# Last expert feed-forward of a gated cross-attention stack: tokens sorted by expert through DRAM, 96 blocks of 128 rows for the two chosen experts

## Chip, cores and metric

The kernel runs on one core of one Trainium2 chip. The metric is the device time of one execution in microseconds. Engine names are those of the profile: PE (TensorE), DVE (VectorE), ACT (ScalarE), POOL (GpSimd) and SP, which issues DMAs.

## What is computed

The input x has 32 x 128 = 4096 rows of 128 numbers, all fp32. Four layers follow each other, each a gated cross-attention and a gated feed-forward of another kind. Only the last feed-forward is touched:

```
h = rmsnorm(layernorm(x)) * norm_w
logits = h @ gate_w.T + gate_b                 # 8 experts
vals, idx = top_k(logits, 2);  wts = softmax(vals)
t1 = einsum('td,efd->tef', h, mlp1_w) + mlp1_b # 256 wide: gate and linear halves interleaved
act = min(g, 7) * sigmoid(1.702 * min(g, 7)) * (clip(l, -7, 7) + 1)
y = einsum('tei,edi->ted', act, mlp2_w) + mlp2_b
x = x + tanh(g_ffn[3]) * (layernorm(x) + sum of wts * y over the two chosen experts)
```

The reference computes y for all eight experts and then takes two of them.

## The kernel before

x stays in SBUF for the whole program, as 32 tiles of 128x128; a group is four tiles (512 rows), so there are NG = 8 groups. Every engine has its own program, written out by hand stage after stage, in the order of `todo`: attention 0, feed-forward 0, attention 1, feed-forward 1 with the token attention, feed-forward 2, attention 2, feed-forward 3. An engine runs its instructions in order, and waits on semaphores that others raise (`wait_ge`). `walk` writes the first and last pair of groups out and loops over those between. The stages meet at the counter `x_written`, which VectorE raises.

In the last feed-forward (`feed_forward3` of each engine) the loops run over 8 groups, and in each over 8 experts. A group's rows are normalised (VectorE L1159 to L1182, POOL L439 to L522), POOL multiplies by the rms factor (L485), TensorE turns the tiles (L977), ScalarE copies them (L704), TensorE makes the logits (L1000) and VectorE picks the two best with 13 small operations and makes the weights (`top2`, L1411 to L1449). Per expert TensorE makes the gate half (L1090) and the linear half (L1093) for 512 rows; VectorE takes the gate half (L1615), ScalarE copies the linear half (L774), VectorE clips it (L1618), ScalarE makes the sigmoid (L779), POOL makes both products (L476, L493), TensorE the down product (L1009), and VectorE adds it to x times the row's weight, zero for six of eight experts (L1460). The biases of the down product are added for all experts at once (L1104, L1623). All the weights lie in SBUF since attention 2 began.

SP's queue carries plain DMAs alone: `load_ctx` (L341), `spread` (L355, L359), the token loads of `token_attention` (L410) behind the spreads of attention 1, and, once `x_written` passes each quarter, four stores of the output (L424). POOL issues no DMA.

## Time and profile before

| | |
|---|---|
| median of 3 runs | 1883.38 us (1877.07 to 1887.72) |
| the profiled execution | 1879.95 us |
| its span, first to last instruction | 1877.0 us |
| granted TensorE clock, mean | 0.921 of 2.4 GHz |
| DMA packets, bytes | 62833, 63.59 MB |

A fp32 product shows as two matmul instructions (passes), a transpose or a bf16 product as one. Busy times of TensorE are modelled at their ends, so of passes back to back the spacing tells more than the mean. A row of a timeline gives start and length in us, and for an instruction that ended an idle time that idle time and who released it. "SPq" is SP's own queue of orders; a DMA's length there is the time to issue it, and the time to landing stands in the list of DMA issues.

### The profile page before, as it was taken

What the parts mean: (1) busy time and instruction counts of PE and PEld (TensorE: products, weight loads), DVE (VectorE), ACT (ScalarE), POOL (GpSimd) and SP (SyncE); (2) the same over time, 40 slices, a digit from 0 to 9 for tenths busy, and PEclk for the clock granted to TensorE, in tenths of its full rate; (3) what the DMA queues carried; (4) which work ended last, traced back from release to release, by engine and by line L of the source; (5) the groups of instructions that cost most, each with busy time, mean ns of one, the idle gap of its engine ahead of it and who ended that gap; (6) DMA issues with size and microseconds to landing.
All of it is one profiled execution on the core that took longest, in us unless ns stands there. A gap on an engine that the chain in (4) does not pass through costs nothing. (4 is left out here: it accounts for less than half of the span.)

```text
span 1877.0 us, 33463 instructions
## 1 busy us (share of the span) xinstructions
PE 1519.4 (81%) x10824; PEld 925.0 (49%) x10824; DVE 1393.7 (74%) x3602; ACT 781.4 (42%) x1314; POOL 511.7 (27%) x559
## 2 busy tenths in 40 slices
PE   3888894488889799889889899935788899778787
PEld 1455552255555465555555455522355556445454
DVE  5777776667776547888887888876567667698997
ACT  1555563145556423334333333422356556333332
POOL 0000000000000003354353443553000000477786
PEclk9998897589999899999999999975999999899998
DMA  7444530254253000000000000004053532000000
GB/s 170 68 70 57 71 53 1 34 145 70 41 69 55 1 1 1 6 1 7 6 0 6 0 7 18 1 0 73 9 70 43 71 47 35 1 1 12 11 12 12
DMA packets 62833, 63.59 MB, mean 34 GB/s; under 512 B 6064, under 2 KB 57776, under 8 KB 62128
## 3 DMA queue, kind: packets, MB, share of 16 engines
q1 hardware_dynamic: 62704, 61.99, 20.3%
q8 instruction: 66, 1.08, 0.2%
q14 instruction: 63, 0.52, 0.1%
HBM read 22.12 MB, written 2.10 MB: 13 GB/s over the span
## 5 line engine op out<-in xcount | busy, mean ns | idle before, releaser
L1208 DVE TENSOR_REDUCE neg_max<-bank 128x4 f32<-128x512 f32 x384 | 260.4, 687 | 114.2 <-PE bank L839 108.0
L653 ACT ACTIVATE probs<-bank 128x512 f32<-128x512 f32 x384 | 229.2, 598 | 237.7 <-PE bank L862 235.3
L1009 PEld LDWEIGHTS bank<-room,area 128*128 128x128 f32 x2048 | 254.7, 199 | 100.2 <-issue 63.0
L439 POOL TENSOR_SCALAR rstd_a<-meanvar 128x4 f32<-128x4 f32 x64 | 17.0, 266 | 1023.5 <-DVE meanvar L1164 1023.5
L1009 PE MATMUL bank<-room,area 128*128 128x128 f32 x2048 | 264.0, 284 | 31.2 <-DVE area L1489 17.3
L729 ACT ACTIVATE work<-bank 128x512 f32<-128x512 f32 (+1 forms) x192 | 114.6, 597 | 358.0 <-PE bank L1034 353.1
L1038 PE MATMUL bank<-xT,room 128*128 128x512 f32 (+1 forms) x384 | 201.1, 606 | 16.2 <-DVE area L1489 16.1
L837 PE MATMUL bank<-mask_b,ident_b 128*128 128x512 bf16 x384 | 158.0, 412 | 66.7 <-DVE neg_max L1208 55.3
L1489 DVE TENSOR_TENSOR area<-work,bank 128x512 f32<-128x512 f32 (+1 forms) x192 | 128.8, 679 | 99.3 <-PE bank L1038 78.2
L1034 PE MATMUL bank<-xT,room 128*128 128x512 f32 (+1 forms) x384 | 198.3, 598 | 0.0
L551 POOL TENSOR_TENSOR prod<-mask_i,work 128x128 f32<-128x128 f32 (+3 forms) x128 | 126.6, 1022 | 156.7 <-DVE mask_i L1550 156.7
L839 PE MATMUL bank<-k_rows,q_rows 96*128 96x256 bf16 x768 | 157.2, 288 | 0.0
L862 PE MATMUL bank<-q_rows,k_rows 128*128 128x128 bf16 x1536 | 156.5, 227 | 0.0
L862 PEld LDWEIGHTS bank<-q_rows,k_rows 128*128 128x128 bf16 x1536 | 124.3, 102 | 62.2 <-issue 15.5
L858 PE MATMUL bank<-ident_b,mask_b 128*128 128x512 bf16 x384 | 154.4, 402 | 0.0
L646 ACT ACTIVATE q_rows<-bank 32x512 bf16<-32x512 bf16 x192 | 113.3, 590 | 95.9 <-PE bank L849 91.7
L874 PE MATMUL bank<-probs,v_aug 128*32 128x128 f32 x3072 | 151.1, 290 | 1.2 <-ACT probs L653 1.0
L1460 DVE SCALAR_TENSOR_TENSOR x<-bank,comb,x 128x128 f32<-128x128 f32 (+1 forms) x512 | 143.0, 339 | 5.5 <-PE bank L1009 3.4
L538 POOL TENSOR_TENSOR probs<-h,work 128x128 f32<-128x128 f32 (+3 forms) x128 | 114.4, 924 | 83.2 <-DVE probs L1530 73.9
L1038 PEld LDWEIGHTS bank<-xT,room 128*128 128x128 f32 (+1 forms) x384 | 68.6, 182 | 117.9 <-issue 85.9
L1182 DVE TENSOR_SCALAR xn<-x,meanvar,rstd 128x128 f32<-128x128 f32 (+1 forms) x192 | 75.6, 456 | 55.2 <-POOL rstd L441 55.0
L839 PEld LDWEIGHTS bank<-k_rows,q_rows 96*128 96x128 bf16 x768 | 79.1, 103 | 55.2 <-issue 13.5
(164 smaller groups left out, 2402.6 us busy)
## 6 DMA issues: line engine op xcount, KB each, us to landing
q_rows<-area SPq DMA_DIRECT2D x144, 128.0 KB
k_rows<-area SPq DMA_DIRECT2D x288, 64.0 KB
ctxT<-ctx_t SPq DMA_DIRECT2D x24, 256.0 KB, 8.0
mask_i<-mask SPq DMA_DIRECT2D x8, 256.0 KB, 8.5
work<-ctx_in SPq DMA_DIRECT2D x8, 256.0 KB, 2.8
out<-x SPq DMA_DIRECT2D x4, 512.0 KB, 3.2
room<-w_down SPq DMA_DIRECT2D x1, 1536.0 KB, 13.8
room<-w_gate SPq DMA_DIRECT2D x1, 1408.0 KB, 6.3
```

Of the source, the lines that this page charges most:

```text
L653: act.activation(probs[j].rearrange("p a b -> p (a b)"), T_BANK[j % 2][:], ACT.Exp).then_inc(exp_done, 1)
L837: pe.matmul(dst[:], ident_b[:], bcast(mask(b, t), 4), start=True, stop=False)
L839: mm = pe.matmul(dst[:, 256 * i:256 * i + 256], q_rows[b][SCORE_ROWS, 2 * j + i, tok], k_rows[b][SCORE_ROWS, :, 2 * j + i, tok], start=Fal ...
L858: pe.matmul(dst[:], mask(b, t), bcast(ident_b[:], 4), start=True, stop=False)
L862: mm = pe.matmul(dst[:, i * P:(i + 1) * P], k_rows[b][:, i % 2, 2 * j + i // 2, tok], q_rows[b][:, 2 * j + i // 2, tok], start=False, stop ...
L874: mm = pe.matmul(O_BANK[32 * i:32 * i + 32, j * P:(j + 1) * P], v_aug[b][:, t, 4 * j + i, :], probs[j][:, i, :], start=True, stop=True)
L1009: mm = pe.matmul(dst[:, t * P:(t + 1) * P], h[:, t * P:(t + 1) * P], w, start=i == 0, stop=i == len(terms) - 1)
L1034: pe.matmul(S_BANK[(3 * e + c) % 2][0:size, :], wg[:, e, at:at + size], xT[b][:], start=True, stop=True).then_inc(gate_filled, 1)
L1038: pe.matmul(T_BANK[(3 * e + c) % 2][0:size, :], wu[:, e, at:at + size], xT[b][:], start=True, stop=True).then_inc(up_filled, 1)
L1208: dve.tensor_reduce(neg_max[:, 4 * j:4 * j + 4], S_BANK[j % 2][:].rearrange("p (h k) -> p h k", h=4), AX.X, ALU.max, negate=True).then_inc ...
L1460: ins = dve.scalar_tensor_tensor(xt, src[:, t * P:(t + 1) * P], comb[cb][:, t, e:e + 1], xt, ALU.mult, ALU.add)
L1489: dve.tensor_tensor(hidden[e % 2][0:size, c, :], work[(3 * e + c) % 2][0:size, :], T_BANK[(3 * e + c) % 2][0:size, :], ALU.mult).then_inc( ...
```

## The change

Only the last feed-forward is rewritten; four DMAs are added before the token attention, and one constant at the start of the program.

- The 4096 rows are worked on in NCH = 4 chunks of 1024 rows (TC = 8 tiles). For each chunk VectorE chooses the two experts of each row (`choose`, 13 chained operations), TensorE counts ranks (`ranks`, 17 bf16 products with a triangular and an all-ones matrix), and VectorE turns them into row addresses and a table of 24 blocks: each block's expert and its place (`put`, 4 chained operations to the addresses, 15 more to the table).
- POOL scatters the chunk's normalised rows to a DRAM buffer `moe_rows` with 16 indirect DMAs of 128 rows, in two halves with the norm chain of a later group between them (`scatter`). Each expert has a region of 1152 rows per chunk; another 3072 rows take the blocks that are empty. The buffer has 4 x 12288 rows of 512 B and is cleared by four DMAs (`clear_rows`) that SP issues before the token loads.
- Then 24 rounds k run, six per chunk, each on a "quad" of four blocks. SP reads each block's address from SBUF into a register (`value_load`) and loads the block (`load`); TensorE turns the blocks (`turn_blk`), reads the four experts' offsets into registers (`value_load` in `up`), multiplies by the weights at these offsets, adds biases with a one-hot bf16 product, turns the hidden rows (`turn_hidden`) and makes the down product (`down_blk`); ScalarE copies between PSUM and SBUF and makes the sigmoid; VectorE clips and multiplies. SP stores the four result blocks to the places they came from (`store`). The two products that POOL made are now VectorE's.
- When a chunk's blocks are stored, POOL gathers them back in 16 indirect DMAs (`gather`; the order on POOL is scatter 0, 1, 2, gather 0, scatter 3, gather 1, 2, 3), and VectorE adds them to x with their weights (`combine3`, 16 operations a chunk).
- The product with the rms factor moves from POOL to VectorE (`group_norm`). The up and down biases are loaded after attention 2 has ended, and split into three bf16 parts by VectorE in eight chained operations (`split_bias`) ahead of the first norm.

The code around the rounds, of SP, POOL, ScalarE, TensorE and VectorE in turn; removed lines are those of the stage described above:

```diff
+TC = 2 * TG
+NCH = NT // TC
+CAP = TC * P + P
+QUAD = 4
+NQ = 6
+NBLK = QUAD * NQ
+REGION = E * CAP + NBLK * P
...
+            def clear_rows():
+                sp.wait_ge(zeros_made, 1)
+                for c in range(NCH):
+                    sp.dma_start(moe_rows[c * REGION:(c + 1) * REGION].rearrange("(p i a) d -> p i (a d)", p=P, a=4),
+                                 bcast(zeros[:], REGION // (4 * P))).then_inc(zeroed, 16)
...
+            def feed_forward3():
+                sp.wait_ge(x_written, NT * 6)
+                sp.dma_start(bias_f[BIAS_ROWS], bias3).then_inc(experts_loaded, 16)
+                sp.wait_ge(zeroed, 16 * NCH)
+                rows_at = {}
+                def load(k):
+                    c, q = divmod(k, NQ)
+                    if q == 0:
+                        sp.wait_ge(table_ready, c + 1)
+                        sp.wait_ge(scattered[c], 16 * 2 * TC)
+                    if k >= 4:
+                        sp.wait_ge(blk_turned, k - 3)
+                    waits_apart(sp)
+                    for j in range(QUAD):
+                        at = sp.value_load(block_i[0:1, c, QUAD * q + j:QUAD * q + j + 1], min_val=0,
+                                           max_val=NCH * REGION - P)
+                        rows_at[k, j] = at
+                        sp.dma_start(blk[k % 4][:, j, :], moe_rows[bass.ds(at, P), :]).then_inc(blk_loaded[k % 4], 16)
+                def store(k):
+                    sp.wait_ge(blk_out, k + 1)
+                    waits_apart(sp)
+                    for j in range(QUAD):
+                        sp.dma_start(moe_rows[bass.ds(rows_at[k, j], P), :], work[2 + k % 2][:, j * P:(j + 1) * P]
+                                     ).then_inc(blk_stored[k % 2], 16)
+                for k in range(NCH * NQ):
+                    load(k)
+                    if k >= 3:
+                        store(k - 3)
+                for k in range(NCH * NQ - 3, NCH * NQ):
+                    store(k)
 
...
-                    lambda: (attention(2, True), load_experts3()), lambda: attention(2, False), lambda: None)
+                    lambda: (attention(2, True), load_experts3()), lambda: attention(2, False), feed_forward3)
...
+                def scatter(c, half):
+                    pool.wait_ge(placed, c + 1)
+                    pool.wait_ge(h3_ready, 2 * c + half + 1)
+                    if c == 0 and half == 0:
+                        pool.wait_ge(zeroed, 16 * NCH)
+                    waits_apart(pool)
+                    for t in range(TG):
+                        for k in range(2):
+                            o = 2 * (TG * half + t) + k
+                            pool.indirect_dma_start(
+                                moe_rows, bass.IndirectOffsetOnAxis(place_i[:, c, o:o + 1].bitcast(mybir.dt.uint32), 0),
+                                h_all[:, TC * c + TG * half + t, :], None).then_inc(scattered[c], 16)
+                def gather(c):
+                    for b in range(2):
+                        pool.wait_ge(blk_stored[b], 16 * QUAD * NQ // 2 * (c + 1))
+                    if c >= 2:
+                        pool.wait_ge(combined, c - 1)
+                    waits_apart(pool)
+                    for o in range(2 * TC):
+                        pool.indirect_dma_start(
+                            y_taken[c % 2][:, o, :], None, moe_rows,
+                            bass.IndirectOffsetOnAxis(place_i[:, c, o:o + 1].bitcast(mybir.dt.uint32), 0)
+                        ).then_inc(gathered[c], 16)
 
                 rms_norm(0)
+                rms_norm(1)
+                rms_norm(2)
+                for c in range(3):
+                    scatter(c, 0)
+                    rms_norm(2 * c + 3)
+                    scatter(c, 1)
+                    if c < 2:
+                        rms_norm(2 * c + 4)
+                gather(0)
+                scatter(3, 0)
+                scatter(3, 1)
+                for c in range(1, NCH):
+                    gather(c)
 
...
+                def take_out(k):
+                    act.wait_ge(blk_down, k + 1)
+                    if k >= 2:
+                        act.wait_ge(blk_stored[k % 2], 16 * QUAD * (k // 2))
+                    act.activation(work[2 + k % 2][:], R_BANK[:], ACT.Copy).then_inc(blk_out, 1)
...
+                take_blk(0)
+                for k in range(NCH * NQ):
+                    c, q = divmod(k, NQ)
+                    if k + 1 < NCH * NQ:
+                        take_blk(k + 1)
+                    if c < 2:
+                        if q == 1:
+                            turned(2 * c + 4)
+                        if q == 3:
+                            turned(2 * c + 5)
+                    gate(k)
+                    if k >= 1:
+                        take_hidden(k - 1)
+                    if k >= 2:
+                        take_out(k - 2)
+                    if c < 2 and q == 4:
+                        gap_weight(c + 2)
+                take_hidden(NCH * NQ - 1)
+                take_out(NCH * NQ - 2)
+                take_out(NCH * NQ - 1)
 
...
+                def turn_blk(k, turns):
+                    pe.wait_ge(blk_loaded[k % 4], 16 * QUAD * (k // 4 + 1))
+                    if k:
+                        pe.wait_ge(blk_taken, k)
+                    pe.wait_ge(f_read, FB[3] + turns)
+                    for j in range(QUAD):
+                        mm = pe.transpose(X_BANK[:, j * P:(j + 1) * P], blk[k % 4][:, j, :], ident[:])
+                    mm.then_inc(blk_turned, 1)
+                weights_at = {}
+                def up(k):
+                    c, q = divmod(k, NQ)
+                    for j in range(QUAD):
+                        b = QUAD * q + j
+                        weights_at[k, j] = pe.value_load(expert_i[0:1, c, b:b + 1], min_val=0, max_val=3 * P * (E - 1))
+                    pe.wait_ge(blk_taken, k + 1)
+                    for half, (bank_, free, filled) in enumerate(((S_BANK, glu_taken, blk_glu),
+                                                                  (T_BANK, blk_lin_taken, blk_lin))):
+                        if k >= 2:
+                            pe.wait_ge(free, k - 1)
+                        for j in range(QUAD):
+                            dst = bank_[k % 2][:, j * P:(j + 1) * P]
+                            pe.matmul(dst, turned_blk[k % 2][:, j * P:(j + 1) * P],
+                                      room[:, bass.ds(weights_at[k, j] + half * P, P)], start=True, stop=False)
+                            hot = expert_hot[BIAS_ROWS, c, QUAD * q + j:QUAD * q + j + 1].to_broadcast([32 * PARTS, P])
+                            mm = pe.matmul(dst, hot, bias_b[BIAS_ROWS, half * P:(half + 1) * P], start=False, stop=True)
+                        mm.then_inc(filled, 1)
+                def turn_hidden(k):
+                    pe.wait_ge(blk_hidden, k + 1)
+                    if k:
+                        pe.wait_ge(blk_hid_taken, k)
+                    for j in range(QUAD):
+                        mm = pe.transpose(O_BANK[:, j * P:(j + 1) * P], hid[k % 2][:, j * P:(j + 1) * P], ident[:])
+                    mm.then_inc(blk_hid_turned, 1)
+                def down_blk(k):
+                    c, q = divmod(k, NQ)
+                    pe.wait_ge(blk_hid_taken, k + 1)
+                    if k:
+                        pe.wait_ge(blk_out, k)
+                    for j in range(QUAD):
+                        dst = R_BANK[:, j * P:(j + 1) * P]
+                        hot = expert_hot[BIAS_ROWS, c, QUAD * q + j:QUAD * q + j + 1].to_broadcast([32 * PARTS, P])
+                        pe.matmul(dst, hot, bias_b[BIAS_ROWS, 2 * P:3 * P], start=True, stop=False)
+                        mm = pe.matmul(dst, work[k % 2][:, j * P:(j + 1) * P],
+                                       room[:, bass.ds(weights_at[k, j] + 2 * P, P)], start=False, stop=True)
+                    mm.then_inc(blk_down, 1)
+                for c in range(2):
+                    turned(2 * c, 0)
+                    turned(2 * c + 1, 0)
+                    logits(c)
+                    ranks(c)
+                turn_blk(0, 4)
+                for k in range(NCH * NQ):
+                    c, q = divmod(k, NQ)
+                    turns = min(2 * c + 4 + (q >= 2) + (q >= 4), 2 * NCH)
+                    if k + 1 < NCH * NQ:
+                        turn_blk(k + 1, turns if q < NQ - 1 else min(2 * c + 6, 2 * NCH))
+                    up(k)
+                    if c < 2 and q in (1, 3):
+                        turned(2 * c + 4 + (q == 3), k + 2)
+                    if k >= 1:
+                        turn_hidden(k - 1)
+                    if k >= 2:
+                        down_blk(k - 2)
+                    if c < 2:
+                        if q == 3:
+                            logits(c + 2)
+                        if q == 5:
+                            ranks(c + 2)
+                turn_hidden(NCH * NQ - 1)
+                down_blk(NCH * NQ - 2)
+                down_blk(NCH * NQ - 1)
 
...
+                def gated(k):
+                    dve.wait_ge(blk_glu, k + 1)
+                    if k >= 2:
+                        dve.wait_ge(blk_sig, k - 1)
+                    dve.tensor_scalar(glu[k % 2], S_BANK[k % 2][:], 7.0, None, ALU.min).then_inc(glu_taken, 1)
+                    dve.wait_ge(blk_lin, k + 1)
+                    dve.tensor_scalar(lin[k % 2], T_BANK[k % 2][:], 8.0, -6.0, ALU.min, ALU.max).then_inc(blk_lin_taken, 1)
+                    dve.wait_ge(blk_lin_taken, k + 1)
+                    step(dve.tensor_tensor(lin[k % 2], lin[k % 2], glu[k % 2], ALU.mult))
...
+                for k in range(NCH * NQ):
+                    c, q = divmod(k, NQ)
+                    gated(k)
+                    if c < 2:
+                        if q == 0:
+                            group_norm(2 * c + 5)
+                        if q == 1 and c == 0:
+                            group_stats(6)
+                        if q == 4:
+                            choose(c + 2)
+                        if q == 5:
+                            put(c + 2)
+                            if c == 0:
+                                group_norm(6)
+                                group_stats(7)
+                    hide(k)
+                    if c >= 2 and q == NQ - 1:
+                        combine3(c - 2)
+                combine3(2)
+                combine3(3)
 
...
```

## Rows read from the trace of the kernel before

**Rows 1.** The page, first part: busy time, share of the span, instructions.

```profile
PE 1519.4 (81%) x10824; PEld 925.0 (49%) x10824; DVE 1393.7 (74%) x3602; ACT 781.4 (42%) x1314; POOL 511.7 (27%) x559
```

**Rows 2.** Busy time by stretch, last feed-forward: us, each engine (count), clock, DMA.

```profile
1606.00:1877.00 271.00, 209.25 (x936) 131.71 (x936) 232.59 (x648) 86.89 (x153) 196.31 (x184) 0.92 0.03 8
```

**Rows 3.** Groups by line and form, 1605 to 1877 us: busy, mean ns, idle before.

```profile
L476 POOL TENSOR_TENSOR probs<-probs,work 128x512 f32<-128x512 f32 x64 | 82.6, 1290 | 49.5 <-DVE probs L1618 49.5
...
L1009 PE MATMUL bank<-room,area 128*128 128x128 f32 x512 | 74.2, 291 | 13.9 <-POOL area L493 13.9
...
L1615 DVE TENSOR_SCALAR work<-bank,cols 128x512 f32<-128x512 f32 x64 | 47.5, 742 | 4.0 <-DVE comb L1449 2.0 <-DVE route L1420 0.9 <-PE bank L1090 0.8
...
L1618 DVE TENSOR_SCALAR probs<-probs 128x512 f32<-128x512 f32 x64 | 42.1, 658 | 11.5 <-ACT probs L774 11.4
L779 ACT ACTIVATE work<-work 128x512 f32<-128x512 f32 x64 | 40.1, 627 | 87.5 <-DVE work L1615 85.0 <-POOL area L493 2.5
...
L1460 DVE SCALAR_TENSOR_TENSOR x<-bank,comb,x 128x128 f32<-128x128 f32 x128 | 35.8, 339 | 3.9 <-PE bank L1009 3.4
```

**Rows 4.** Timeline where the last feed-forward begins: start, length, instruction, idle before.

```profile
1605.71 0.29 DVE L1253 TENSOR_TENSOR x<-x,tgbo 128x128 f32<-128x128 f32 x1
...
1607.42 0.23 POOL L439 TENSOR_SCALAR rstd_a<-meanvar 128x4 f32<-128x4 f32 x1 [78.08 <-DVE meanvar L1164]
...
1609.96 0.75 DVE L1600 SCALAR_TENSOR_TENSOR x<-xn,gates,x 128x512 f32<-128x512 f32 x1
1611.05 1.04 POOL L485 TENSOR_TENSOR h<-xn,rms 128x512 f32<-128x512 f32 x1 [0.17 <-POOL rms L522]
...
1614.27 1.88 PE L1000 MATMUL bank<-wr,xT 128*128 128x8 f32 x8 [0.84 <-ACT xT L704]
...
1616.18 0.19 DVE L1411 TENSOR_TENSOR route<-bank,rows 128x32 f32<-128x32 f32 x1 [5.47 <-PE bank L1000]
...
1618.71 0.19 DVE L1437 TENSOR_TENSOR route<-rows,route 128x32 f32<-128x32 f32 x1
```

**Rows 5.** How orders to the DMA queue are issued: ns, min/median/max, by line.

```profile
L341 SPq DMA_DIRECT2D ctxT<-ctx_t x24: 336/350/543, 4.9 to 1532.4; - x24
L341 SPq FUSED_REGOPS  x12: 43/46/56, 126.3 to 1532.2; - x12
...
L359 SPq DMA_DIRECT2D k_rows<-area x288: 602/613/1720, 27.8 to 1566.0; - x144
```

**Rows 6.** The page, last part: DMA issues, KB each, us from issue to landing.

```profile
room<-w_down SPq DMA_DIRECT2D x1, 1536.0 KB, 13.8
...
ident<-consts_in SPq DMA_DIRECT2D x1, 64.0 KB, 2.5
...
wr<-w_router SPq DMA_DIRECT2D x1, 4.0 KB, 1.6
```

**Rows 7.** Timeline of TensorE: passes back to back at full and at half clock.

```profile
1592.33 0.39 PE L862 MATMUL bank<-q_rows,k_rows 128*128 128x128 bf16 x4
...
1592.55 0.61 PE L886 MATMUL bank<-ident,heads_t 128*128 128x128 f32 x4
...
1701.68 1.05 PE L1009 MATMUL bank<-room,area 128*128 128x128 f32 x8
...
1869.90 2.08 PE L1009 MATMUL bank<-room,area 128*128 128x128 f32 x8 [1.87 <-POOL area L493]
```

**Rows 8.** Busy time by stretch, a thinly used stretch after the first feed-forward.

```profile
301.00:378.00 77.00, 25.24 (x103) 13.30 (x103) 50.83 (x116) 8.72 (x14) 4.24 (x7) 0.51 0.18 25
```

**Rows 9.** Timeline of the end: last expert add and last output store.

```profile
1872.01 1.12 DVE L1460 SCALAR_TENSOR_TENSOR x<-bank,comb,x 128x128 f32<-128x128 f32 x4 [2.64 <-PE bank L1009]
...
1873.36 0.37 SPq L424 DMA_DIRECT2D out<-x  x1
```

**Rows 10.** Timeline: token loads issued, and their first reader on POOL.

```profile
595.03 1.00 SPq L410 DMA_DIRECT2D work<-ctx_in  x2
...
723.12 3.31 POOL L538 TENSOR_TENSOR probs<-h,work 128x128 f32<-128x128 f32 x4 [1.23 <-DVE h L1182]
```

More of the change, by code:

```diff
@@ L51 @@
 CH1 = [(0, 128), (128, 128), (256, 96)]
+TC = 2 * TG
[5 more added lines that the diff above has]
+REGION = E * CAP + NBLK * P
+PARTS = 3
+BIAS_ROWS = slice(0, 32 * PARTS)
 MASKED = -float(2.0 ** 100)
@@ L496, in feed_forward3 @@
-                rms_norm(0)
-                def body(gp, first, last):
-                    for gr, b, is_first, left in groups(gp, first, last):
-                        for e in range(E):
-                            if e >= 1:
-                                hide(E * gr + e - 1, e - 1, DB3 + 9 * gr + e - (1 if e >= 3 else 2))
-                            elif not is_first:
-                                hide(E * gr - 1, 7, DB3 + 9 * gr - 2)
-                            if e == 1 and left >= 1:
-                                rms_norm(gr + 1)
-                            products(E * gr + e, e)
@@ L1114, in feed_forward3, with turned, logits @@
-                walk(pe, body)
-                for e in (E - 2, E - 1):
-                    finish(E * NG + e - E, e, DB3 + 9 * NG + e - E)
+                pe.wait_ge(experts_loaded, 16 * 8)
+                pe.wait_ge(bias_split, 1)
+                def turned(p, blocks):
+                    if blocks:
+                        pe.wait_ge(blk_taken, blocks)
+                    turn(3, p)
+                def logits(c):
+                    for half in range(2):
+                        pe.wait_ge(f_read, FB[3] + 2 * c + half + 1)
+                        if c and half == 0:
+                            pe.wait_ge(chosen_ready, c)
+                        for t in range(TG):
+                            at = (TG * half + t) * E
+                            mm = pe.matmul(N_BANK[:, at:at + E], xT[half][:, t * P:(t + 1) * P], wr3[:],
+                                           start=True, stop=True)
+                    mm.then_inc(logits_filled, 1)
```

354 lines of the change are left out of this document (212 added, 142 removed).

## Prediction

> **What bounds the kernel now.** I read the page's busy shares first: over the whole run TensorE leads with 81% and VectorE follows with 74% [rows 1]. The change lies in the last feed-forward, so next I read busy time by stretch. That stage begins when attention writes its last row at 1606.0 us and ends with the span at 1877.0: 271 us, in which VectorE is busy for 232.6, TensorE for 209.3, POOL for 196.3 and ScalarE for 86.9 [rows 2, 4]. VectorE comes closest to a bound: per group of 512 rows and expert it takes the gate half (64 x 0.742 = 47.5 us in all), clips the other half (42.1) and adds the expert's output to x (256 x 0.339, twice the 35.8 of the row shown, = 72) [rows 3]. All of it goes with 8 groups x 8 experts = 64 rounds, so a round costs 271/64 = 4.2 us. The median of three runs is 1883.4 us; the profiled execution took 1880.0, its span 1877.0. I add to this execution, so my figure is some 3 us below what the median would give. A difference of 0.5% (9 us) is about what a measurement can tell from none.
>
> **What the change does to engine time.** The 64 rounds go. In their place 24 rounds ("quads") of four 128-row blocks run, and around them stand a sort and a gather. Per quad TensorE issues 8 one-pass fp32 transposes, 12 fp32 products of two passes each, and 12 bf16 bias products. Eight fp32 passes take 1.05 us, one of them some 0.29, so a pass adds (1.05-0.29)/7 = 0.108; four bf16 passes take 0.39, so 0.054 each [rows 3, 7]. That is 32 x 0.108 + 12 x 0.054 = 4.1 us at the full clock and 8.2 at the half clock, where the same eight passes take 2.08 [rows 7]. VectorE: 0.742 x 2 from PSUM, two 512-wide SBUF products at some 0.66 (L1618's mean), waits 0.4: 3.2 us. Its adds fall from 256 to 64, which saves 65 us. By busy time alone the stage would shrink. What decides is what a quad waits for.
>
> **The loop through the SP queue.** SP's program is load(k), then store(k-3). TensorE's round k begins with the turn of quad k+1, so needs load(k+1). On SP that stands behind store(k-3), which waits for ScalarE's copy of quad k-3. That copy reads what TensorE made as the *last* work of round k-1 (down_blk). So four input buffers exist, yet the load that round k needs first is ordered only after round k-1 has ended. From round 3 to round 22, 20 times, the legs add up:
> - SP leg. Hand-over and copy, 0.3 + 0.6 + 0.2 = 1.1 us (the copy by L779's 0.627 [rows 3]). Four stores: a contiguous store or load of 128 runs is issued in 0.35 us at L341, plus two address instructions of 0.046, so 0.45 each, 1.8 in all [rows 5]. The strided spreads take 0.61, the upper bound. Four loads, each behind a register load from SBUF: 4 x (v + 0.45). Landing of the last: a 64 KB load took 2.5 us, a 4 KB load 1.6; I take 2.2 [rows 6].
> - The register load v (value_load) is not in this trace. It cannot be less than a register operation, 0.05 us, and I bound it above by a whole 4 KB transfer, 1.6 us [rows 5, 6]. The nearest row is the issue of one DMA, also sequencer work that reaches across the chip, 0.35; the value must come back besides, so I take 0.5. SP leg: 1.1 + 1.8 + 3.8 + 2.2 = 8.9 us.
> - TensorE leg. Wait 0.2; four register loads of its own, 4 x 0.5 = 2.0, in its queue behind the turn; addresses 0.3; array work between 4.1 and 8.2. With 4 to 8 us of work in a round of 18 the array is thinly used; at a third busy the granted clock was 0.51, nearly always the lower level, 1.2 GHz [rows 8]. The work comes in bursts, though, so I take the middle, 6.2. Leg: 8.7 us.
>
> A round is 17.6 us; 20 rounds are 352 us. ScalarE and VectorE (3.2 us, in rounds with routing some 13) fit beneath it at no cost; if the loop were short, they and TensorE would set some 7 us.
>
> The Trainium skill ("DMA: Bandwidth & Descriptors", Latency and other measured facts) gives a floor of about 600 ns for loading a register; no row here shows it. By it v is 0.6, and eight such loads in 20 rounds make the forecast 16 us later.
>
> **Before the first quad.** Bias: its DMA is issued only when attention is done (2.7 us by [rows 6]) and VectorE splits it in eight chained steps of some 0.55: 7.1 us. Two groups normalised in turn: from 1605.9 to 1610.7, plus a product of 0.7: 5.6 each, 11.2 [rows 4]. Transposes, copy and logits: 4.1 us from 1612.1 to 1616.2 before, 4.5 for two. Choice: 13 chained operations took 2.7 us, 3.1 for twice the width [rows 4]. Ranks (17 bf16 products, cold) 2.4 and places 1.5. So rows have places at 1606 + 30 = 1636. Then POOL scatters 16 times, with a norm chain of 3.6 us between [rows 4]. An indirect DMA is not in this trace: below, 0.35 as SP's issue; above, two passes of a 128x512 tensor by POOL, 2.6; I take one pass, 1.3 (L476) [rows 3, 5]. 16 x 1.3 + 3.6 = 24.4, landing 2.5: 1663. Load(0) 3.8 + 2.2, load(1) 3.8: round 0 starts at 1673, 67 us into the stage. Rounds 0 to 2 have loads ahead: 7 + 8 + 9 = 24 us.
>
> **After it.** Round 23 and the last turn and down 13; copy, stores, landing 5.4; gather(3) 16 x 1.3 + 2.5 = 23.3; combine 16 x 0.339 + 0.5 = 5.9; output store 3.7, as from 1873.3 to the end of the span [rows 3, 9]. Together 51 us. The other 96 indirect DMAs (125 us at 1.3) lie beside the quads. Both 16s on the path move by 32 us for each microsecond of price.
>
> The Trainium skill (same page, Anatomy of one DMA) gives 2.0 us fixed plus bytes by 436 GB/s for a DMA from GpSimd, mostly completion, which overlaps when many are in flight. If it did not overlap, 2.15 instead of 1.3 in 32 of them would be 27 us more.
>
> **Elsewhere.** Clearing 4 x 12288 rows of 512 B writes 25.2 MB from SP, ahead of the token loads now issued at 595 us and first read at 723 [rows 10]. At the rate of the 1536 KB load (13.8 us, with its start) it is 226 us, 98 late [rows 6]; an idle queue should do better, so I take nothing, upper bound 98. The extra constant at the start and the turns inside quads of chunks 0 and 1: 5 us. All other stages stay.
>
> **Sum.** 67 + 24 + 352 + 51 + 5 = 499 us against 271: +228. 1880 + 228 = **2108 us**, 12% slower. With every term low (v 0.05, full clock, landing 1.6) a round is 11.2 us and the time 1980; with v 1.6, strided issue and half clock it is 31 and 2376.
>
> **Rivals.**
> - *Faster: the loop costs nothing.* Place: SP's store(k-3). If outputs were ready when SP reaches it, quads would go at the engines' pace, TensorE 4.1 + 4v. With v 0.05, full clock, cheap scatter (0.4) a quad takes 5.4: 57 + 130 + 35 = 222 us, 1831 in all. Decision point: 147 + 20R = 271 gives R = 6.2 us a round. Against it: the legs above exceed that even at their lowest, 11.2; it needs the order of the queues to be other than read. 4%. The same without the loop but at v 0.5: some 7 us a quad, near 1885, 3%.
> - *POOL sets the pace.* At 3.5 us an indirect DMA, POOL has 128 x 3.5 + 35 = 483 us of work and the 32 on the path add 70: about 2180. For it: POOL is slow per operation here (0.23 us for four elements a lane, rows 4). The Trainium skill ("SBUF — State Buffer", the "DVE blocks DMA" trap) adds that VectorE's fast mode can keep GpSimd from writing descriptors. 8%.
> - *The clearing stalls the tokens*: up to +98, so 2206, with the rest as forecast. 7%.
> - *It does not do what it says*: the static 96 blocks run whether full or empty, so work never falls below 24 quads. That is in the sum.
>
> **Chances.** Forecast (R from 13 to 23) 78%, POOL 8, clearing 7, no loop 7 (faster 4, the same 3). Range: R 13 to 23 gives 2016 to 2216; the bounds of v and of the rivals widen it to 1985 to 2265. Faster by over 0.5% 0.04, within 0.5% 0.03, slower 0.93.
>
> **What would show it.** In the changed profile: SP's longest total wait is its stores on ScalarE's output copy; TensorE waits about 20 times some 9 us for blocks' landing; the mean clock of the stage is nearer 0.6 than 0.92; quads follow each other at 16 to 19 us; register loads on SP and TensorE near 0.5 us; first block load issued near 1663. The prediction is wrong if TensorE's waits for blocks are short, or if POOL's queue is solid between the first scatter and the last gather, or if a stage before 1606 us has moved by over 10 us.

## The result, and the profile after

The changed kernel takes 2114.09 us (median of 4 runs, 2110.17 to 2115.08) against 1885.37 us before (4 runs on the same chip): ratio 1.1218, 95% interval 1.1192 to 1.1245. The forecast was 2108 us, 12% slower. The profiled execution took 2113.85, its span 2112.1.

First the page's first part and the busy time of the last feed-forward in three stretches: attention's last row (1604.6 us) to just before the first store of a quad, the waiting rounds, the rest. They answer to [rows 1, 2].

```profile
PE 1522.4 (72%) x11108; PEld 980.0 (46%) x11108; DVE 1308.5 (62%) x3375; ACT 761.5 (36%) x1271; POOL 467.3 (22%) x552
...
core 0: us, PE busy (x) PEld busy (x) DVE busy (x) ACT busy (x) POOL busy (x), PEclk, DMA share, GB/s
1604.60:1693.00 88.40, 32.51 (x194) 29.00 (x194) 49.60 (x182) 10.75 (x17) 54.58 (x74) 0.55 0.12 38
1693.00:2060.00 367.00, 164.38 (x920) 143.31 (x919) 78.96 (x182) 50.81 (x83) 82.05 (x86) 0.66 0.15 44
2060.00:2112.00 52.00, 15.95 (x108) 14.45 (x108) 18.70 (x59) 5.44 (x9) 15.10 (x16) 0.63 0.29 81
```

Attention ends within 1.4 us of where it did before, so the earlier stages, clearing included, did not move. The stage takes 507.5 us where it took 271. It is no longer short of an engine: VectorE is busy for 147 us where it was for 233, POOL for 152 where it was for 196. In the middle stretch nobody is busy for half of the time, TensorE included (164 of 367 us). So the time lies in waits. This is the table of waits over 1693 to 2060 us (who waited, for whom, total, times, longest), and the same for SyncE's queue:

```profile
DVE area L1881 <- PE bank L1264: 238.0, 19, 14.9
ACT area L866 <- PE bank L1244: 180.3, 20, 9.6
PEld bank L1244 <- DMA k_rows<-moe_rows: 171.9, 20, 9.2
PE bank L1244 <- DMA k_rows<-moe_rows: 168.5, 20, 9.0
```

```profile
SPq L91 <- ACT work L879: 249.2, 20, 16.8
```

Every engine waits, each for the next one round the ring: VectorE for TensorE, TensorE for the loaded blocks (20 times, 8.4 us on average), SyncE for ScalarE's copy of the output (20 times). Only the order of the queues tells which link is superfluous. One round in time (TensorE's bf16 bias products and weight loads, POOL and some VectorE lines left out):

```profile
1806.38 0.44 PE L1284 MATMUL bank<-room,work 128*128 x2
...
1806.86 0.60 ACT L879 ACTIVATE work<-bank 128x512 f32<-128x512 f32 x1 [0.74 <-PE bank L1284]
1807.60 1.78 SPq L481 DMA_DIRECT2D moe_rows<-work  x4
...
1810.19 3.64 SPq L475 DMA_DIRECT2D k_rows<-moe_rows  x4
...
1815.38 1.11 PE L1244 MATMUL bank<-ident,k_rows 128*128 128x128 f32 x4 [8.56 <-DMA k_rows<-moe_rows]
1816.54 0.69 ACT L866 ACTIVATE area<-bank,cols 128x512 f32<-128x512 f32 x1 [9.08 <-PE bank L1244]
1818.16 0.79 PE L1261 MATMUL bank<-room,area 128*128 x2 [1.66 <-ACT area L866]
...
1826.38 0.60 ACT L879 ACTIVATE work<-bank 128x512 f32<-128x512 f32 x1 [0.26 <-PE bank L1284]
1827.12 1.78 SPq L481 DMA_DIRECT2D moe_rows<-work  x4
```

The reader is to see one chain in which only one link works at a time: down projection (L1284), copy (L879), four stores (L481), four loads (L475), landing, turn (L1244), up projection (L1261), down projection. TensorE stands still for 8.56 us of it. From the stores at 1694.0 to those at 2069.0 there are 20 such rounds in 375.0 us, 18.75 each; 17.6 was forecast.

The reads of registers were the price the trace of before did not have. This is what lines 472 (SyncE) and 1253 (TensorE) issue, ns as min/median/max:

```profile
L472 SPq TENSOR_LOAD <-k_rows x96: 263/268/494, 1659.2 to 2055.1; - x96
L472 SPq FUSED_REGOPS  x96: 152/152/185, 1659.7 to 2055.4; - x96
L472 SPq SEQ_ASSERT  x96: 18/18/37, 1660.0 to 2055.6; - x96
```

```profile
L1253 PEldq TENSOR_LOAD <-k_rows x96: 293/298/578, 1669.8 to 2067.3; - x96
```

### The profile page after: what moved, and what is told of

Read it like the earlier page. It is cut to its first block and busy times, and to the rows that moved or that the text cites. A ratio compares the mean times of both kernels' runs of the same rounds, so it can differ in the third digit from the quotient of the medians.

```text
span 2112.1 us, 34421 instructions
## 1 busy us (share of the span) xinstructions
PE 1522.4 (72%) x11108; PEld 980.0 (46%) x11108; DVE 1308.5 (62%) x3375; ACT 761.5 (36%) x1271; POOL 467.3 (22%) x552
## 3 DMA queue, kind: packets, MB, share of 16 engines
q0 software_dynamic: 4096, 8.40, 1.3%
## 5 line engine op out<-in xcount | busy, mean ns | idle before, releaser
L1139 PEld LDWEIGHTS bank<-room,area 128*128 128x128 f32 x1536 | 187.3, 198 | 56.4 <-issue 41.7
L1139 PE MATMUL bank<-room,area 128*128 128x128 f32 x1536 | 191.0, 283 | 16.8 <-DVE area L1686 16.8
L1881 DVE TENSOR_SCALAR area<-bank 128x512 f32<-128x512 f32 x24 | 16.6, 691 | 265.4 <-PE bank L1264 265.4
L1244 PE MATMUL bank<-ident,k_rows 128*128 128x128 f32 x96 | 25.7, 420 | 180.4 <-DMA k_rows<-moe_rows 180.4
L1261 PE MATMUL bank<-room,area 128*128 x384 | 116.6, 448 | 38.4 <-ACT area L866 23.8
```

The costliest lines, as they stand in the source:

```text
L1139: mm = pe.matmul(dst[:, t * P:(t + 1) * P], h[:, t * P:(t + 1) * P], w, start=i == 0, stop=i == len(terms) - 1)
L1261: pe.matmul(dst, turned_blk[k % 2][:, j * P:(j + 1) * P], room[:, bass.ds(weights_at[k, j] + half * P, P)], start=True, stop=False)
```

## Experiments

Four groups of kernels ran, each group on one chip, and the chips turned out to differ in one thing (below), so I compare rounds within a profile as well as times. A round is the distance between two turns of a quad (the line of `pe.transpose(X_BANK..., blk...)`), and I give the median of the 20 waiting ones, with their mean where it differs. The numbers in brackets behind a time are its ratio to the kernel before, measured on the same chip, and the 95% interval of that ratio.

### One part of the loop at a time

**The store one round later.** SyncE only:

```
-                    if k >= 3:
-                        store(k - 3)
-                for k in range(NCH * NQ - 3, NCH * NQ):
+                    if k >= 4:
+                        store(k - 4)
+                for k in range(NCH * NQ - 4, NCH * NQ):
                     store(k)
```

> One index changes: SyncE stores quad k-4 after the loads of quad k, where it stored quad k-3. Loop theory: the loads of quad k+1 now stand behind a store whose data are ready one PE round earlier, so SyncE's leg (8.6 us from the end of the down projection to the first turn of the next quad) lies beside a whole PE round. Two rounds can then not be shorter than 8.6 + 10.2, that is 9.4 us each, and one not shorter than TensorE's own 9.1 to 11 us: a round falls from 18.75 to about 10.2 us, 20 rounds give back 170 us, and the time is about 1944 (1900 to 1980, the lower end if TensorE's clock rises with its share of work). PE's wait of 180 us for the loaded blocks goes almost wholly. Rival, a round is long because its work is long (POOL, VectorE or the register loads): the same work is issued in another order, the round stays near 18.75 us and the time within 10 us of 2114. Rival, the loads themselves are slow in landing: half a round at most is saved, above 2030.

Measured: 1987.78 us (1.0552, 1.0511 to 1.0594). The median round is 10.0 us, as expected; the mean is 12.4, because five rounds took 17 to 23 us (below). Without their extra 55 us the time would lie in the expected range, which it missed by 8 us. TensorE's waits for blocks fell from 168.5 us to 29.5 (over 1693 to 1935 us):

```profile
PE bank L1244 <- DMA k_rows<-moe_rows: 29.5, 10, 4.5
```

No work was taken away and nothing faster was put in. An index moved by one takes 126 us off the changed kernel's first median, and 164 off its repeat below. Neither rival, work that is long in itself or loads that land slowly, allows for that.

**TensorE's reads early.** A new `offsets(k)` holds the four `value_load` of `up(k)` and stands ahead of `turn_blk(k + 1)`.

> TensorE reads its four weight offsets into registers before it waits for the quad to turn, instead of after the turn. They then lie in the wait of 8.6 us. Loop theory: four reads at about 0.3 us and their sequencer work, 1.3 to 1.9 us of each round's path, are hidden in 20 rounds: 26 to 38 us less, about 2082 (2072 to 2092). Rival, the reads cost nothing because they run beside the four turns that are still in the array: no change, 2114 within 4 us.

**SyncE's reads early.** A new `places(k + 1)` holds the four `value_load` of `load(k + 1)` and stands ahead of `store(k - 3)`.

> SyncE reads the four row offsets of quad k+1 into registers right after the loads of quad k, so before it waits for the output copy, instead of between the transfers. Loop theory: the four loads then go out 0.33 to 0.45 us apart instead of 1.10, the last one 2.6 to 3.1 us earlier in each of 20 rounds: 52 to 62 us less, about 2057 (2045 to 2070). Rival, what spaces the loads is the address work of each transfer and not the read of the register: at most 1 us a round, above 2094.

**TensorE kept busy.**

```
+FILL = 70
...
+                    for _ in range(FILL if 14 <= k < 23 else 0):
+                        pe.matmul(N_BANK[:, 384:512], ident_b[:], ident_b[:], start=True, stop=True)
                     if k + 1 < NCH * NQ:
```

> In rounds 14 to 22 TensorE runs 70 BF16 multiplications of 128 columns into an unused part of a PSUM bank before it waits for the next quad; nothing else is touched and the result is not used. At full clock they take 70 x 0.053 = 3.7 us, at half clock 7.5, both within the wait of 8.6. Theory, part of a round's length is that TensorE idles in it and then does its quad at 1.2 GHz: the granted clock of these rounds rises from 0.66 toward 1 and the array part of their leg falls from 8.2 toward 4.1 us. The leg is 9.1 to 11 us with the VectorE, ScalarE and register parts in it, so 2 to 3 us a round in 9 rounds: 18 to 27 us less, about 2092, and rounds 3 to 13 of the same profile stay at 18.75. Rival, the array's speed is hidden by other waits within the leg: below 5 us in all.

Measured: 2105.97 with TensorE's reads early, 2112.41 with SyncE's, 2154.28 with the filler. Against 2114 all three miss. But each of these profiles had four rounds some 7 to 11 us longer than the rest, the later store's had five, 7 to 13 us longer, and the changed kernel's own had none. So the changed kernel ran again, unedited, with the next group:

> The changed kernel as it is, run beside the next kernels on one chip. In the runs so far four rounds of each edited kernel (the ones with turns 10, 14, 16 and 22) are about 10 us longer than the rest, which no round of the changed kernel's own profile is; VectorE and ScalarE stand still in them while POOL issues sixteen indirect transfers. If those edits brought the stalls, this one has none and takes 2114 within 4 us. If the chip or the placement of the program brings them, this one has them too and takes about 2150.

Measured: 2151.42 us (2144.44 to 2152.61), with the same four long rounds (27.5, 25.8, 27.1 and 27.3 us; the median is 19.2). The edits did not bring them. Against 2151 the three read: TensorE's reads early 45 us less, a median round of 16.9; SyncE's 39 less, also 16.9; the filler 3 more, which is no difference beside single times of 2144 to 2158. (The first group's chip was another one than the repeat's. Both show the long rounds, and the medians of the rounds agree with the times. The last feed-forward alone, from attention's end to the end of the span, takes 546.7 us in the repeat's profile, 506.8 with TensorE's reads early and 507.0 with SyncE's.)

- TensorE's four reads were worth 2.3 us a round, more than the 1.3 to 1.9 expected. From the start of the turn to the start of the up projection it is now 0.9 us where it was 2.8, so 1.9 of them are the reads. The other 0.4 lies in the array: from the start of the up projection to the end of the down projection it takes 6.84 us on average where the repeat took 7.25 (15 rounds each, the long ones left out). Products stand 0.64 us apart at the lower clock level and 0.33 at the upper, and in some of these rounds the change to 0.33 comes earlier. What brings it earlier is not shown. The rival, that the reads run beside the turns, falls.
- SyncE's were worth 2.0 a round, less than the 2.6 to 3.1 expected. With the reads gone the four loads go out in 1.93 us, (1.93 - 0.33)/3 = 0.53 apart, where they were (3.64 - 0.33)/3 = 1.10 apart. A read thus costs 0.57 us, and the transfer itself 0.53, not 0.33: the address takes the rest. Four reads are 2.3 us, and from the end of the down projection to the next turn the rounds did get 2.3 us shorter (8.72 to 6.41). The array part took 0.3 longer (7.25 to 7.59), and so 2.0 are left.
- The filler failed as an experiment:

```profile
2001.12 4.07 PE L1299 MATMUL bank<-ident_b 128*128 128x128 bf16 x70
2010.79 1.12 PE L1245 MATMUL bank<-ident,k_rows 128*128 128x128 f32 x4 [5.60 <-DMA k_rows<-moe_rows]
```

The 70 products ran at close to the spacing of the full clock (4.07/70 = 0.058 us each), but TensorE then stood still for 5.6 us and the turns were back at the half clock (1.12 us for four, which take 0.61 at the full clock [rows 7]). That work had been put at the wrong end of the wait. What the half clock costs a round is not measured by this run.

**The turn at the end of the round.** TensorE calls `turn_blk(k + 1)` after `down_blk(k - 2)`, ScalarE's `take_blk(k + 1)` moves behind `take_out(k - 2)`, and the counts of turned groups are adjusted to it; SyncE's order stays.

> TensorE turns quad k+1 at the end of round k, after the down projection of quad k-2, instead of at its start; ScalarE's copy of the turned quad moves with it. SyncE's order is as in the changed kernel: store k-3, then loads of k+1. Loop theory: the store waits for the down projection of quad k-3 at the end of TensorE's round k-1 and its consumer, the turn, has moved back by the up projection and the turn of the hidden quad, 6 to 8 us of work that now lie beside SyncE's leg of 8.6 us. A round becomes the longer of TensorE's 9 to 10 us and 8.6 + about 4 us for down projection and turn: about 12 us instead of 18.75, so 20 rounds give back 135 us: about 1980 (1950 to 2010), plus 40 if this kernel has the four stalls of 10 us. Rival, TensorE's wait only moves to the end of the round and is as long as before: within 15 us of the changed kernel.

Measured: 1987.45 us (1.0565, 1.0501 to 1.0629), 164 less than the repeat, a median round of 10.0 (12 was expected) and a mean of 12.2 where the repeat has 20.4. So the same 8 us a round come back by moving the consumer instead of the producer. Both engines still do the same work at their own speed; what went is the dependence that put one's work behind the other's.

**Later store and early reads together** (SyncE and TensorE).

> The store one round later (round 9.9 us in its run where nothing stalled) with both engines' register reads put ahead of their waits. Loop theory: with the store later the loop is no longer SyncE's alone; what is left is SyncE's issue work, four loads and four stores, 1.8 + 1.8 us and the reads 2 to 3 us, and TensorE's round of 6.5 to 8 us. Early reads take 1.5 to 2 us of TensorE's path out: a round of about 8 us, 20 rounds give back 2 us each against the later store alone: about 1950 (1925 to 1975) where that alone took 1988. Rival, rounds of 9.9 us are set by POOL's indirect transfers or VectorE: no change against 1988.

Measured: 1948.34 us (1.0349, 1.0281 to 1.0417), 39 us below the later store alone, the 2 us a round that were expected (the median went from 10.0 to 8.1, the mean is 10.4). POOL or VectorE as the limit of rounds of 10 us falls.

### The long rounds

In a long round VectorE and ScalarE both stand still, though TensorE has handed over. VectorE and ScalarE in the repeat's first one:

```profile
1805.74 0.69 DVE L1881 TENSOR_SCALAR area<-bank 128x512 f32<-128x512 f32 x1 [14.06 <-PE bank L1264]
1818.47 0.69 DVE L1883 TENSOR_SCALAR probs<-bank 128x512 f32<-128x512 f32 x1 [12.04 <-remote]
```

```profile
1806.46 0.63 ACT L873 ACTIVATE area<-area 128x512 f32<-128x512 f32 x1 [4.55 <-issue]
1818.52 0.60 ACT L885 ACTIVATE work<-bank 128x512 f32<-128x512 f32 x1 [11.43 <-remote]
```

TensorE's last product of the round starts at 1809.85, and what VectorE waits for was made before. Both engines go on within 0.05 us of each other here, and the profile names no releaser ("remote"). All four stalls begin inside one of POOL's runs of sixteen indirect transfers (1796.0 to 1815.8 the first) and end 1.0 to 2.8 us behind it; the runs of eight before them (1755.9 to 1780.0) brought none. So I paced POOL: four transfers, then a wait for the next quad's output copy.

> The changed kernel, with POOL held back: of the sixteen indirect transfers of a gather (groups 0 to 2) and of the last scatter it issues four per round, each four behind a wait for the next quad's output copy, so that no more than 5 us of indirect transfers go out without a break. Theory, a run of about eight and more of them is what makes VectorE and ScalarE stand still (four times about 10 us in the repeated run of the changed kernel): the four long rounds go and the time is 2114 (2105 to 2120). Rival, every indirect transfer holds the two engines a little and they only show where the run is long: the same 40 us spread over sixteen rounds, 2140 to 2155. Rival, the stalls have nothing to do with indirect transfers: four long rounds stay, near 2151.

Measured: 2114.48 us (2107.91 to 2117.35), no long round. That would fit, but the next kernel ran unpaced on the same chip, with runs of sixteen and more, and has none either. So does the changed kernel's first profile. Chips (or what is placed where in them) differ in this, and pacing is not shown to help. It costs nothing while rounds are 18.7 us long (2114.48 against 2114.09 unpaced).

### Taking the loop away

**Stores by ScalarE.** SyncE's `store` goes; ScalarE reads the four offsets and issues the stores right behind `take_out(k - 2)`, so no load stands behind a store.

> The four stores of a quad are issued by ScalarE, right behind its own output copy and four register reads, instead of SyncE; SyncE issues the loads alone and waits only for buffers. Loop theory: no load stands behind a store any more, so TensorE never waits for a quad, and the round is TensorE's own 9 to 10 us or ScalarE's: its four or five copies 2.6 us, its reads about 1.6 and its four issues 1.8, 6 us. A round of about 9.5 us instead of 18.75: 20 rounds give back 185 us of the 2151 (1945 to 1985). Rival, the round is as long because data come late from DRAM whoever issues them: within 20 us of 2151.

Measured: 1899.70 us (1.0104, 1.0062 to 1.0145), 215 us below the paced kernel of the same group and below the expected 1945 to 1985: TensorE's own round had been put at 9 to 10 us. TensorE waits for no block any more (no such line is left in its waits), the median round is 7.3 us, the mean 8.2, and TensorE's granted clock rises with it, from 0.66 to 0.89, though nothing was done for it:

```profile
1690.00:1835.00 145.00, 114.19 (x877) 104.67 (x876) 74.88 (x177) 42.49 (x75) 73.58 (x77) 0.89 0.34 96
```

**All of it.** Stores by ScalarE, TensorE's and ScalarE's single reads ahead of their waits, POOL paced.

> Stores by ScalarE, register reads of TensorE and ScalarE ahead of their waits, and POOL's indirect transfers in fours. Loop theory and the prediction's point of no difference, 6.2 us a round: TensorE's round is 5.5 to 6 us of array work at full clock and 1.2 to 1.6 us of register reads, 7 to 7.5 us, so 20 rounds take 145 us where the changed kernel took 375: 2114 - 230 = 1884 without the long rounds (1865 to 1905), no difference from the kernel before. If the long rounds stay, about 40 more. If VectorE or POOL (32 indirect transfers of 1.26 us in the middle rounds) set the pace, a round is 8 us or more and the time above 1905.

Measured: 1892.13 us (1.0040, 1.0011 to 1.0069). Rounds of 7.26 us on average; 7 to 7.5 and 1884 were expected. A round of 7.3 us leaves the kernel a little slower than before, so the point at which the change breaks even lies below that. (POOL is hardly held back here: with short rounds most copies it waits for are made already, and it issues 20 and 16 transfers with no pause of 1 us.)

**One read for four values.** With the stores by ScalarE and the reads early, each engine loads four neighbouring offsets by one instruction:

```
+def four(nc, engine, ap, top):
+    return nc.values_load_multi_w_load_instructions(ap, engines=[engine], min_val=0, max_val=top)[1]
...
+                def offsets(k):
+                    c, q = divmod(k, NQ)
+                    at = four(nc, mybir.EngineType.PE, expert_i[0:1, c, QUAD * q:QUAD * (q + 1)], 3 * P * (E - 1))
+                    for j in range(QUAD):
+                        weights_at[k, j] = at[j]
+
                 def up(k):
                     c, q = divmod(k, NQ)
-                    for j in range(QUAD):
-                        b = QUAD * q + j
-                        weights_at[k, j] = pe.value_load(expert_i[0:1, c, b:b + 1], min_val=0, max_val=3 * P * (E - 1))
```

> Stores by ScalarE and early register reads as before, POOL unpaced, and each engine reads the four offsets of a quad with one instruction for a row of four values instead of four instructions. Loop theory: what is left of a round is issue work on the path, four reads of 0.3 to 0.5 us each on TensorE and the same on ScalarE; one read for four takes 1 to 1.5 us off each round where the reads still show (most rounds of 7.3 us go to about 6.2, those with routing work stay). Against stores by ScalarE with single reads (1892 with early reads) 20 rounds give 15 to 30 us: 1862 to 1878, which is faster than the kernel before (1883) by 0.3 to 1.1%. Rival, one instruction for four values takes as long as four (1.1 us): 1892, slower by 0.5%. If VectorE and ScalarE stand still in the long runs of indirect transfers on this chip, 40 us more in this kernel.

Measured: 1861.51 us (6 runs; 0.9874, 0.9843 to 0.9905), 20 us and about 1% faster than the kernel before (1881.92). The instruction for four takes about as long as one for one did:

```profile
L90 SPq TENSOR_LOAD <-k_rows x24: 293/304/537, 1662.4 to 1802.6; - x24
L90 PEldq TENSOR_LOAD <-k_rows x24: 327/334/972, 1667.7 to 1818.4; - x24
L90 ACTq TENSOR_LOAD <-k_rows x24: 306/314/607, 1690.0 to 1832.9; - x24
```

In rounds without routing work TensorE has no gap left. Three turns in a row, and the stretch:

```profile
1779.70 0.60 PE L1256 MATMUL bank<-ident,k_rows 128*128 128x128 f32 x4
...
1784.54 0.60 PE L1256 MATMUL bank<-ident,k_rows 128*128 128x128 f32 x4
...
1789.38 0.60 PE L1256 MATMUL bank<-ident,k_rows 128*128 128x128 f32 x4
```

```profile
1690.00:1820.00 130.00, 112.05 (x966) 106.34 (x966) 80.80 (x187) 48.34 (x85) 76.68 (x82) 0.93 0.41 117
```

Such a round takes 4.84 us, all of it TensorE's. The mean of the 20 is 6.6, because rounds with norms, logits and choices still take up to 13. POOL is unpaced in this kernel, so against "all of it" two things differ.

**The same, POOL paced.**

> The same with POOL's indirect transfers of the gathers and the last scatter in fours behind the output copies. On a chip where the kernel without this shows stalls of VectorE and ScalarE of 10 us, breaking up the runs of transfers takes them away (20 to 45 us faster than the one without), if a long run of them is what it takes; if each transfer stalls the engines a little, it changes nothing. On a chip where the other shows no stalls, both take the same within 5 us.

Measured: 1873.00 us (0.9962, 0.9930 to 0.9994). Neither profile has a stall of the two engines, so the question of the long rounds stays open here too. As above, the waits hardly break up POOL's transfers: 28 and 20 go out with no pause of 1 us. Against "all of it" only the reads of four differ (and the chip): 1892.13 became 1873.00, the mean round 7.26 became 7.0. Against the unpaced kernel it is 11 us slower.

The earlier stages are the same code in all these kernels, yet their attention ends anywhere from 1593.5 to 1614.6 us, for reasons that no run shows. So for small steps the last feed-forward by itself is of use, from there to the end of the span:

| profile | last feed-forward, us | attention ends at |
|---|---|---|
| before | 271.0 | 1606.0 |
| the change | 507.5 | 1604.6 |
| stores by ScalarE | 302.8 | 1593.5 |
| all of it | 281.3 | 1609.1 |
| the same with reads of four | 268.8 | 1614.6 |
| reads of four, POOL unpaced | 260.8 | 1607.8 |

Each row is one profiled execution, so the differences are rough. By them the early reads (with the pacing) save 21 us where the times show 8, the reads of four save 12.5, pacing costs 8, and the fastest kernel wins 10 us in the stage that was changed. The rest of its 20 us is not shown to come from the change.

## Why the prediction was right

**The mechanism held.** SyncE's program puts load(k+1) behind store(k-3), whose data are the last thing TensorE makes in round k-1. The later store and the later turn break just this and give back 164 us each. Stores on ScalarE take it away and give 215.

**The sum by terms**, in us, forecast against measured:

| term | forecast | measured |
|---|---|---|
| before the first round | 67 | 65.2 (1604.6 to the turn at 1669.8) |
| rounds 0 to 2 | 24 | 23.5 (to the end of the down projection at 1693.3) |
| rounds 3 to 22 | 20 x 17.6 = 352 | 20 x 18.75 = 375.0 |
| after them | 51 | 43.8 |
| extra turns and the start | 5 | in the rounds |

The sum, 499, is 8.5 us short of the 507.5 measured, and that it comes so close is partly luck: rounds 3 to 22 with the extra turns in them took 18 us more than forecast, the other stretches 9.5 less.

- **SP leg** 8.9 forecast, 8.65 measured on average, from the end of a down projection to the next turn. (TensorE's own wait is 8.4, since it makes logits and ranks in four of these legs.) In the round shown: hand-over and copy 0.8 (forecast 1.1), stores 1.8, from there to the last load's issue 4.4 (3.8), landing 1.55 (2.2). Two misses cancel: reads and addresses were too cheap, the landing too dear.
- **TensorE leg** 8.7 forecast, 18.75 - 8.65 = 10.1 measured, the whole miss of the loop: 1.4 x 20 = 28 us, less 5 for the SP leg. In rounds 12 to 22, which have no work for later groups, it is 10.0 on average: 1.7 from turn to up projection with the four reads (forecast 2.5 with the wait) and 8.3 in the array (6.2). Rounds 3 to 11 take only 0.3 more, so the work for later groups was not dearer than the 5 us put down for it. The array work has two misses of about 1 us each. One is the price of a pass. A product with its bias product was put at 2 x 0.108 + 0.054 = 0.27 us at the full clock, and they stand 0.33 apart there and 0.64 at the half clock. This is the round that begins at 2001.93, where the level changes:

```profile
2005.32 0.31 PE L1264 MATMUL bank<-k_rows 96*128 96x128 bf16 x1
2005.42 0.74 PE L1261 MATMUL bank<-room,area 128*128 x2
2005.96 0.31 PE L1264 MATMUL bank<-k_rows 96*128 96x128 bf16 x1
...
2010.57 0.22 PE L1283 MATMUL bank<-k_rows 96*128 96x128 bf16 x1
2010.63 0.44 PE L1284 MATMUL bank<-room,work 128*128 x2
2010.90 0.22 PE L1283 MATMUL bank<-k_rows 96*128 96x128 bf16 x1
```

So a quad needs 4.84 us at the full clock (the rounds without a gap above), not 4.1, and some 9.5 at the half clock, an estimate from 12 x 0.64 and the eight turns. The middle of these would be 7.2. The other miss is the clock: every round starts at the half clock, the four turns in 1.12 us, and comes back to the full one only in its last part (the last 2.8 us of the 7.8 of this round, 1 to 3 us in the others). That makes 8.3 us of the 7.2.
- **The register read.** 0.5 was taken for v, 0.57 measured in SyncE's path, of which the load instruction is 0.27; on TensorE four reads took 1.9, so 0.48 each. The Trainium skill's floor of about 600 ns ("DMA: Bandwidth & Descriptors", Latency and other measured facts) fits the whole of a read, with its register operations, and not the instruction.
- **The indirect DMA.** 1.3 forecast; 0.95 busy and mostly 1.25 to 1.26 apart. That is why start and end came so close. It also closes "POOL sets the pace": POOL works 82 us in the 367 of the middle stretch. That transfers in flight overlap, as the prediction took for granted, the trace shows: each lands 2.3 to 2.5 us after its issue (medians), and the next goes out after 1.25. The starvation by VectorE that the prediction named beside this rival leaves a small trace at most: 13 of the 128 took 1.1 to 1.6 us instead of 0.95, each of them beside a VectorE instruction that combines two tensors in SBUF (others ran beside such at 0.95). That is 5 us in all.
- **After the rounds** 43.8 instead of 51: from there to the first gather 14.2 (18.4 forecast), the gather until the last landing 21.3 (23.3), the adds 4.4 (5.9), the rest 3.9. The adds were priced by the mean duration of one, 0.339, but they overlap: 35.8 us of busy time for 128 of them [rows 3] and 4.4 for 16 both give 0.28 each. (The prediction's "256 x 0.339" would be 87; the 72 beside it is the busy time, 256 x 0.28, and the saving from 256 to 64 adds is 54 us by it, not 65. Neither enters the sum.)
- **Clearing.** Taken at nothing, and nothing it was: attention ends at 1604.6 against 1606.0. (The 226 us of its upper bound should be 221: 1536 KB are 1.573 MB.)
- **"The same without the loop but at v 0.5: some 7 us a quad, near 1885"** was tried as "all of it": 7.26 us and 1892. "**The loop costs nothing**, decision point 6.2" needed another order and cheaper reads. Built, it gives 6.6 us and 1861. That is on the fast side although 6.6 is above 6.2, since the stretches around the rounds measured 132 us and not the 147 of that sum ((271 - 132)/20 = 6.9). That rival's 5.4 us a quad was reached in the rounds without routing work (4.84), not on average.

What is open: what stalls VectorE and ScalarE for 10 us on some chips; and what moves the end of attention by up to 21 us between kernels whose earlier stages are the same.

## What to carry to other kernels

When every engine is half idle, write down for each queue what stands ahead of the instruction that the bound engine waits for, and how late *its* data come. Buffers do not help if the order in the queue ties the next load to the last output. Move the store back by one turn of the pipeline or give it to the engine that makes its data. Then count the sequencers' own work: four register reads one by one took 1.9 to 2.3 us, a quarter of a round of 7 to 8 us, and the load instruction for a row of four takes about what one for a single value does. When several edits miss by the same amount, run the unedited kernel again beside them. And judge steps of 1% by the stage that was changed as well as by the whole time.

## What the runs showed that I had not expected

- One register-load instruction for a row of four neighbouring values takes 0.30 to 0.33 us on three engines; one for a single value takes 0.27 to 0.30.
- The same kernel took 2114 us on one chip and 2151 on another, beside a kernel before that took 1885 and 1882. Some 32 of the 37 us are four stalls of VectorE and ScalarE during runs of indirect DMAs.
- TensorE's granted clock rose as the loop was broken: 0.66 in rounds of 18.75 us, 0.89 in rounds of 8.2, 0.93 in rounds of 6.6. The quad that took 8.3 us of array time on average in the first takes 4.84 without a gap in the last, so breaking a wait paid twice. Work that ended 5.6 us before the turns (the filler) did not keep the clock up.
